# Attention with routed experts on one core: row places computed earlier, a third row per batch start on VectorE, output additions first, filler transposes, and new orders on all five engines

## The reference

```
xn  = layernorm(x)                                  # per token
q,k,v = xn Wq', xn Wk', xn Wv'                      # 32 query heads, 8 key heads, head size 128
q,k = rotary(q), rotary(k)
attn = softmax(causal(q k' / sqrt(128))) v          # 4 query heads share a key head
a   = attn Wo'
s   = softmax(xn router_w + router_b) + router_bias # 16 experts in 4 groups
keep the 2 groups with the largest maxima, then the 2 largest experts in them -> gate
y   = sum over experts of gate * ((silu(xn w1 + b1) * (xn w2 + b2)) w3 + b3)
z   = (silu(xn sw1 + sb1) * (xn sw2 + sb2)) sw3 + sb3
out = x + a + y + z
```

## Time and profile before

| what | value |
|---|---|
| median of 3 runs | 907.06 us (906.69 to 907.95) |
| the profiled execution, its own time | 905.59 us |
| its span | 903.8 us |
| PE busy | 888.5 us, 98% |
| DVE / ACT / POOL busy | 677.7 / 431.2 / 526.5 us |
| the loop over heads 1 to 6 | about 107.3 us a round |

### The profile page before, as it was taken

One profiled execution on the slowest core, in us unless ns is written; L12 is line 12 of the kernel. 1 busy time (PEld: TensorE's weight loads), 2 busy tenths in 40 slices (PEclk: granted clock), 3 DMA queues, 4 the chain that ended last, 5 costly groups with the idle time before them and its releaser, 6 DMA issues.

```text
span 903.8 us, 17478 instructions
## 1 busy us (share of the span) xinstructions
PE 888.5 (98%) x5066; PEld 762.2 (84%) x5066; DVE 677.7 (75%) x1614; ACT 431.2 (48%) x1083; POOL 526.5 (58%) x638
## 2 busy tenths in 40 slices
PE   8997999999999999999999999999999999999998
PEld 7786887888888888888888889888888888888886
DVE  6688876687767876768767786768776787676886
ACT  3504543554535644454554545445453564454543
POOL 5923786565654765538554575356565476543663
PEclk9999999999999999999999999999999999999999
DMA  9910223143223532335222443224322252230242
GB/s 329 319 47 15 92 94 123 42 131 121 88 76 86 172 95 79 90 99 168 87 87 76 114 163 87 75 81 126 123 87 75 89 172 94 80 92 22 84 150 94
DMA packets 52161, 97.73 MB, mean 108 GB/s; under 512 B 5920, under 2 KB 17824, under 8 KB 52128
## 3 DMA queue, kind: packets, MB, share of 16 engines
q1 hardware_dynamic: 49568, 88.94, 31.7%
q0 software_dynamic: 2560, 8.39, 2.8%
HBM read 74.76 MB, written 22.54 MB: 108 GB/s over the span
## 4 chain that ended last, share of the span: by engine, by line
PE 92%; DVE 5%; issue 1%; ACT 1%; DMA 0%; POOL 0%; SPq 0%; DVEq 0%
PE bank L1992 10%; PE bank L1990 10%; PE bank L1991 10%; PE bank L2190 7%; PE bank L2129 7%; PE bank L2131 6%; PE bank L2130 6%; PE bank L2226 6%; PE bank L2222 6%; PE bank L2223 6%; PE bank L2206 4%; PE bank L2203 4%; PE bank L2204 4%; PE bank L2251 1%; PE bank L2176 1%
## 5 line engine op out<-in xcount | busy, mean ns | idle before, releaser
L636 POOL TENSOR_SCALAR prob<-prob,rsum 128x128 f32<-128x128 f32 (+3 forms) x256 | 143.9, 582 | 89.8 <-DVE rsum L1480 89.1
L876 ACT ACTIVATE prob<-bank,nmax 128x128 f32<-128x128 f32 (+3 forms) x256 | 133.7, 528 | 113.9 <-DVE nmax L1474 111.3
L1474 DVE CUSTOM_DVE_ANT_0 bank<-bank,causal 128x128 f32<-128x128 f32 (+3 forms) x256 | 122.8, 501 | 35.5 <-PE bank L1992 33.7
L1502 DVE TENSOR_TENSOR pT_lo<-bank,pT_hi 128x512 fp32r<-128x512 f32 x160 | 109.1, 684 | 29.0 <-ACT pT_hi L896 28.6
L896 ACT ACTIVATE pT_hi<-bank 128x512 fp32r<-128x512 f32 x160 | 95.0, 596 | 67.1 <-PE bank L2190 53.4
L2222 PE MATMUL bank<-wo_lo,oT_hi 128*128 128x512 f32 x256 | 106.2, 415 | 0.0
L2129 PE MATMUL bank<-xT_hi,wq_lo 128*128 128x512 f32 x256 | 104.7, 409 | 1.5 <-DVE v_lo L1458 1.4
L619 POOL TENSOR_TENSOR w_lo<-w_raw,w_hi 128x1024 fp32r<-128x1024 f32 x31 | 74.3, 2398 | 52.7 <-ACT w_hi L931 52.7
L2131 PE MATMUL bank<-xT_hi,wq_hi 128*128 128x512 f32 x256 | 101.1, 395 | 0.0
L2226 PE MATMUL bank<-wo_hi,oT_lo 128*128 128x512 f32 x256 | 100.7, 393 | 0.0
L2130 PE MATMUL bank<-xT_lo,wq_hi 128*128 128x512 f32 x256 | 100.6, 393 | 0.0
(11 more groups left out here) (219 smaller groups left out, 2326.5 us busy)
## 6 DMA issues: line engine op xcount, KB each, us to landing
w_raw<-w SPq DMA_DIRECT2D x31, 512.0 KB, 3.5
wq_raw<-wq SPq DMA_DIRECT2D x32, 256.0 KB, 4.1
wo_raw<-wo SPq DMA_DIRECT2D x32, 256.0 KB, 2.8
xg<-x_slots SPq DMA_DIRECT2D x31, 256.0 KB, 3.5
w_raw<-w SPq DMA_DIRECT2D x31, 256.0 KB, 2.8
eb<-b SPq DMA_DIRECT2D x31, 256.0 KB, 3.9
y_slots<-eb SPq DMA_DIRECT2D x31, 256.0 KB, 2.5
x_slots<-pairs SPq DMA_DIRECT2D x3, 2048.0 KB, 16.0
```

Of the source, the lines that this page charges most:

```text
L636: last = nc.gpsimd.tensor_scalar(row, row, rsum[:, stat(b, i, h)], 1.0, ALU.mult, ALU.mult)
L876: last = nc.scalar.activation(prob[n % 2][:, h, 0:P * (i + 1)], bank[S_BANKS[use % 2]][:, 256 * k:256 * k + P * (i + 1)], ACT.Exp, bias=nm ...
```

## The change

The multiset of calls in the lists of the heads stays the same, save for what is named here.

1. Of the rows of batch 0, blocks 0, 1 and 2 are normalised on DVE and block 3 on ACT. For batch 1 it stays at two and two. A helper `wait_row` finds the semaphore of a row for PE and POOL.
2. The additions of the shared expert's result to row blocks 0 to 3 (`add_down`) all stand ahead of the choice of groups.
3. `count_blocks` and `first_blocks` leave the list of the first head on DVE. The first stands behind `lo_v(0, 0, 1)` ahead of the rotary steps of head 0, the second behind the first of these steps. `ranks` on PE moves with them, into the query projection of head 0.
4. `keep_busy(g, k)` on PE issues k transposes of the identity into a bank that holds nothing then; for g = 0 only: 9 behind the first scores, 5 ahead of `scores(0, 0, 1, 0)`.
5. All the lists of the heads on all five engines are in another order. In the list of the loop on PE `transpose_x` of the head's first tile is now first. `place_x(0, 0)` on POOL stands third among the calls of the first head that issue something, instead of eighth, and `place_x(0, 2)` behind the addition for the next head's queries; on ACT the `hi_wo` calls of the first head stand later.

```diff
+        DVE_ROWS, ACT_ROWS = (0, 1, 2, 4, 5), (3, 6, 7)
...
-                for n in (TB * b + 2, TB * b + 3):
+                for n in ACT_ROWS[b:2 * b + 1]:
                     nc.scalar.activation(xn[:, n, :], y[:, n, :], ACT.Identity, bias=lnt[:, 5, n:n + 1],
...
-                for n in (TB * b, TB * b + 1):
+                for n in DVE_ROWS[3 * b:3 * b + 3]:
                     nc.vector.tensor_scalar(xn[:, n, :], y[:, n, :], mv[:, n, 0:1], lnt[:, 2, n:n + 1],
...
             hidden(3)
-            for n in range(2):
+            for n in range(TB):
                 add_down(n)
...
-            for n in range(2, TB):
-                add_down(n)
...
             lo_v(0, 0, 1, FIRST_KV_BANKS[1])
+            count_blocks()
             for h in range(G):
                 turned = first_rot[h % 2]
                 turn_q1(0, 0, h, FIRST_Q_BANKS[h], turned)
                 turn_q2(0, 0, h, FIRST_Q_BANKS[h], turned)
+                if h == 0:
+                    first_blocks()
...
-                    (count_blocks, first_blocks, row_slots, row_gates, experts_of_tiles)[k]()
+                    (row_slots, row_gates, experts_of_tiles)[k]()
...
                 for c in range(HC):
                     project_q(0, 0, h, c, FIRST_Q_BANKS[h])
+                    if (h, c) == (0, 2):
+                        ranks()
...
-            def first_ranks(g):
+            def keep_busy(g, k):
 
                 if isinstance(g, int) and g == 0:
-                    ranks()
+                    for _ in range(k):
+                        nc.tensor.transpose(bank[OT_BANK][:, 0:P], ident[:, :], ident[:, :])
...
                 scores(g, 0, 0, 0)
-                first_ranks(g)
+                keep_busy(g, 9)
                 project_kv(g, 1, 0, 0)
                 scores(g, 0, 0, 1)
                 project_kv(g, 1, 0, 1)
+                keep_busy(g, 5)
                 scores(g, 0, 1, 0)
...
             def first_head(g):
                 exps(g, 0, 0, 0)
-                hi_wo(g, 0)
                 exps(g, 0, 0, 1)
-                hi_wo(g, 1)
                 hi_v(g, 1, 0)
```

More of the change, by code:

```diff
@@ L1185, in last_head @@
                 hi_pT(g, 1, 3, 3)
[L1186 removed]
+                exps(g, 1, 1, 0)
                 hi_oT(g, 1, 3)
@@ new lines, in first_head @@
+                transpose_k(g, 1)
+                values(g, 0, 1, 1)
+                transpose_p(g, 0, 2, 1)
+                project_out(g, 0, 0, 2)
+                project_q(g, 1, 2, 0)
+                project_q(g, 1, 2, 1)
+                project_q(g, 1, 2, 2)
+                project_q(g, 1, 2, 3)
+                transpose_p(g, 0, 2, 2)
+                scores(g, 1, 0, 0)
+                values(g, 0, 2, 0)
+                project_out(g, 0, 0, 3)
+                values(g, 0, 2, 1)
+                project_q(g, 1, 3, 0)
@@ new lines, in first_head @@
+                project_q(g, 1, 3, 1)
+                transpose_p(g, 0, 3, 0)
+                project_q(g, 1, 3, 2)
+                project_q(g, 1, 3, 3)
+                transpose_p(g, 0, 3, 1)
+                values(g, 0, 2, 2)
+                project_out(g, 0, 1, 0)
+                project_out(g, 0, 1, 1)
+                project_kv(g + 1, 0, 0, 0)
+                scores(g, 1, 0, 1)
+                values(g, 0, 3, 0)
+                project_kv(g + 1, 0, 0, 1)
+                transpose_p(g, 0, 3, 2)
@@ new lines, in first_head @@
+                project_q(g + 1, 0, 0, 1)
+                project_out(g, 0, 2, 2)
+                project_out(g, 0, 2, 3)
+                project_q(g + 1, 0, 0, 2)
+                scores(g, 1, 2, 1)
+                scores(g, 1, 2, 2)
+                project_out(g, 0, 3, 0)
+                project_q(g + 1, 0, 0, 3)
+                scores(g, 1, 2, 3)
+                transpose_p(g, 1, 1, 0)
+                values(g, 1, 0, 0)
+                project_out(g, 0, 3, 1)
+                project_kv(g + 1, 0, 1, 0)
@@ new lines, in first_head @@
+                project_out(g, 0, 3, 2)
+                project_kv(g + 1, 0, 1, 1)
+                transpose_p(g, 1, 1, 1)
+                project_out(g, 0, 3, 3)
+                scores(g, 1, 3, 0)
+                scores(g, 1, 3, 1)
+                project_q(g + 1, 0, 1, 0)
+                project_q(g + 1, 0, 1, 1)
+                project_q(g + 1, 0, 1, 2)
+                values(g, 1, 1, 0)
+                project_q(g + 1, 0, 1, 3)
+                project_out(g, 1, 0, 0)
+                scores(g, 1, 3, 2)
```

1296 lines of the change are left out of this document (618 added, 678 removed).

## The result

The changed kernel took 916.38 us (median), the kernel before 907.23 on the same chips. One of the four executions of the changed kernel took 3516 us; the ratio leaves it out and goes by the other three, 915.79 to 916.58: 1.0098, 95% interval 1.0078 to 1.0118. It is slower by 1%, outside of the range given. The profiled execution took 916.19 us, its span is 914.4, 10.6 more than before.

What follows compares the result with a forecast made beforehand. PE, busy 98%, was taken to bound the kernel. Terms -1.0 (start to 92), -1.3 (to 160), 0 (fillers), 0 (loop), +0.6 (last head) summed to -1.7: median 907.06 to about 905.3, range 902.6 to 908.9.

Steps and rivals of the forecast that it cites:

- The loop: Six rounds, 160 to 824 us: PE barely idle, can only lose; taken 0, bounds 0 and +0.65 a round, +3.9.
- Rival (c): Loop: each round's query projection meets a missing v_lo or kT_lo; 0.65 a round, +2.2 in all, 909.3; chance 0.15.
- Start: First rows normalised, edit 1: PE's 0.63 wait for xT_hi shrinks by some 0.34; taken -0.3, bounds 0 to -0.63.
- Output additions: Shared expert, edit 2: the 0.98 wait at 49.96 goes with the slow start of the matmul behind it; -1.1.
- Row places: DVE at 60 to 73 us, edit 3: count_blocks and first_blocks use up PE's lead; later waits shrink, row_slots takes back 0.2.
- the wait behind the table load: PE's wait at 77.60 in the first head stays, since a table load of 1.28 stands ahead of the first exps.
- the lead at 92: Start and edits 2 and 3 together: -1.0 at 92 us; wrong if not between 0.5 and 1.5.
- Fillers: First head, edit 4: fourteen transposes fit inside PE's idle time; taken 0, bounds 0 and +0.2.
- Second batch: First head, 92 to 160 us, edit 5: waits of 0.65 and 1.11 mostly shrink; -1.3, bounds -2.1 and +1.
- T1: Experiments' theory that the loop's new orders alone cost the time; it had the old-loop kernel 4.5 us faster than before.
- Last head: Edit 5 at the end: one wait of 1.6 for POOL's normalise, less waits that go; +0.6, bounds -1.5 to +1.6.

Runs made afterwards that it cites:

- A: Loop wait of PE's transposes for a bank lo_pT must read; changed kernel with hi_pT and lo_pT moved ahead of exps and maxima: round 108.85 (-0.76).
- B: Loop wait of project_out for y, the output bank; changed kernel with add_out(g,1,0) moved behind maxima(g,1,3,2): round 108.72 (-0.89).
- C: Loop wait of the query projection for kT_lo; changed kernel with ACT's hi_wo(g,3) moved behind hi_kT(g,1): round 109.52 (-0.1).
- The swap kernel with the first head of the kernel before: The kernel before with the changed kernel's loop lists on all five engines: 916.67 us against 904.23, ratio 1.0137, round 109.55.
- the one with the additions alone: The kernel before with all four output additions ahead of the choice of groups, nothing else: 905.08 us against 906.23, ratio 0.9989.
- the first head alone: The changed kernel with the kernel before's lists for the loop and the last head: 901.30 us against 904.77, ratio 0.9961.
- A, B and C moved: The changed kernel with four calls of the loop moved, for all three waits: 904.45 us against 904.23, ratio 1.0000.
- the kernel with the blocks late: The run with start and first head alone changed, with count_blocks and first_blocks moved behind all four rotary steps: 901.99 us against 901.30, ratio 0.9967.

## Why the prediction was wrong

It said 905.3 and the time was 916.4. The failed step is "**The loop.** ... Taken: 0. Bounds: 0 and +0.65 a round". A term put at nothing costs 2.28 us a round and 13.7 in all; with the old loop lists in its place the kernel is at 0.9984 of the one before, -1.6 us, where the sum without the loop was -1.7. That these two agree is partly luck: in the traces the terms without the loop come to -3.1, not -1.7. Step by step:

- Loop. I compared how much PE work lies between calls that depend on each other, found most distances longer, and took that for safety. Two things were wrong with it. I never set the distances against the length of the chain in the new order, which depends on what stands ahead of each link on ACT and DVE: the wait A comes from ACT standing at `exps` with a ready `hi_pT` behind it, and no distance on PE shows that. Nor did I look at what POOL does beside DVE: in the changed loop (160 to 824 us) 24 of 49 q_lo begin while POOL runs an elementwise instruction, and take 1.20 us in the mean; before it was 13 of 50, and 0.71. And the list of dependent pairs was short: it had no pair for the banks' way back, a transpose into a bank that `lo_pT` has yet to read (A) and an output projection into the bank that `add_out` has yet to empty (B). C is the one that I named, transposed keys to the next projection, and it is the smallest, 0.3 us a round in the trace; that moving its call gives anything is not shown. Rival (c) was right that there would be waits in every round, but its place was the query projection, which is C; at 0.65 a round it was too dear for C, and the two waits that cost most were in no rival.
- Bounds. "It can only lose" was in the text; an upper bound of one wait a round, of the smaller of the two sizes in the earlier trace rows, for lists of up to 158 calls in new order on five engines, had nothing behind it. The loop is run six times, so an unmended 0.3 us there outweighs any term of the start.
- Start, -0.3: right in size. First transposes to first product 2.37 us for 2.62; the wait of 0.63 is 0.36. The first transposes themselves came 0.14 later.
- Output additions, -1.1: right in kind, 1.35 alone.
- Row places, "-1.4 becomes +0.2 at 73": right, +0.39 at the key projection (73.35 for 72.96). The replay held up to the query projection, which came at 79.49 for the forecast 79.55, and the wait behind the table load stays as said: from the first scores to `scores(0, 0, 1, 0)` it takes 6.64 us in both kernels, and the fillers only hide it. The mis-sized part is what follows. I took 0.2 back for row_slots, and 0.6 more was gained, since this wait of the kernel before went:

```profile
89.77 0.44 PE L1990 MATMUL bank<-kT_hi,q_lo 128*128 128x384 f32 x1 [0.59 <-ACT prob L876]
```

So the lead at 92 is 1.9 and not 1.0, outside of the 0.5 to 1.5 that I had set as a sign of being wrong.
- Fillers, 0: right. The rule of the Trainium skill that I set beside it ("TensorE: Matmul & The Clock Gate", Part 4, about 275 ns for a transpose) would have made it +1.6; measured were 0.11 from start to start, and 0.27 us is how long one of them takes, so its figure is a duration here and not what one more costs.
- Second batch, -1.3: the trace gave -2.2, but the cause was misread. Both waits of the earlier trace rows come behind a DVE instruction that starts 1.2 and 1.3 us after PE's last matmul for it had ended. The swap kernel with the first head of the kernel before has neither (its window 130 to 160 below), the one with the additions alone has only one, of 0.62. So they do not follow from the order: they differ between traces of the same first head. That T1's -4.5 became -1.6 may have the same reason, if the kernel before runs without these waits on the chip where it takes 904.23 for 907.23. This is not shown, since that chip has no trace of it; and the first head alone gained 3.5, so how much of the -2.2 a timed run holds is left open.

```profile
130.00:160.00 30.00, 30.00 (x158) 25.16 (x157) 21.64 (x45) 11.80 (x29) 21.41 (x29) 1.00 0.31 116
```

- Last head, +0.6: right in place, +1.0 in size. The forecast had one wait of about 1.6 for POOL; there are three, 0.98 together, for the lo_pT behind combine_two and for POOL's normalise:

```profile
895.54 0.50 PE L2204 MATMUL bank<-pT_lo,v_hi 128*128 128x512 f32 x1 [0.43 <-DVE pT_lo L1504]
896.19 0.41 PE L2188 MATMUL bank<-ident,prob 128*128 128x128 f32 x2 [0.15 <-POOL prob L640]
897.01 0.44 PE L2188 MATMUL bank<-ident,prob 128*128 128x128 f32 x2 [0.40 <-POOL prob L640]
```

That step and the first head's up to 79.5 were replays, call by call, of what three engines have ahead of them; the loop's was not, and this is the difference between the steps that held and the one that fell.

What stays open: with A, B and C moved a round is 107.90, 0.57 above the old one, which no run takes apart; how much of A and B is the order of DVE and ACT alone and how much is POOL's splits beside q_lo; whether C is worth anything; and what makes the second batch's late starts come and go.

## What to carry to other kernels

Where an order is rewritten in a loop, replay the loop first, on every engine that hands something to the bound one, and include the buffers' way back (who must have read the bank before it is written again): busy shares and distances on the bound engine alone show neither. Look also at which instructions of GpSimd the new order puts beside VectorE's. An engine at half load can hold up one at 98% by waiting at the wrong call with a ready one behind it; look for idle time with a ready successor. And a wait that appears once in one trace is no term of a sum until a second kernel with the same lists shows it too.

## What the runs showed of the hardware

A DVE instruction that reads SBUF can be held until an instruction of POOL that runs beside it has ended. In the kernel with the first head alone, DVE and then POOL:

```profile
64.18 0.84 DVE L1386 TENSOR_TENSOR per_expert<-per_expert 128x16 f32<-128x16 f32 x1
63.97 1.01 POOL L669 TENSOR_TENSOR rot<-rot 128x384 f32<-128x384 f32 x1
```

In the kernel with the blocks late the same instruction, with POOL idle, takes 0.17 (at 75.92), and a one-input instruction on 128x16, also 0.17 elsewhere, is held:

```profile
73.17 0.95 DVE L1373 TENSOR_SCALAR iota<-iota 128x16 f32<-128x16 f32 x1
73.09 1.00 POOL L669 TENSOR_TENSOR prob<-prob 128x384 f32<-128x384 f32 x1
```

Both end 0.03 to 0.04 us behind POOL's. The first is 0.67 us on DVE's chain that the sum for `first_blocks` (1.05) did not have. Long instructions are held as well: in the loop of the changed kernel every q_lo (two inputs, 128x384) that begins 0.1 us or more after the start of an elementwise instruction of POOL that is still running ends 0.40 to 0.42 us behind that one's end, up to 2.45 us after its own start, and none of the others takes over 0.56. It goes the other way too: POOL's q_first takes 0.46 at 63.08 in the kernel with the blocks late, and 0.83 at 67.22 in the one with the first head alone, where a q_lo of DVE had begun 0.04 us ahead of it. Not every DVE instruction is held: in the same kernel a one-input TENSOR_REDUCE (L1385, at 63.73) takes its usual 0.42 while q_first runs.

The Trainium skill ("GPSIMD Engine Reference", 1. Specifications) says that GpSimd's SBUF interfaces are shared with VectorE and contended by its instructions with two SBUF inputs or in a 2-port mode. The trace agrees for two inputs; in which mode the one-input instruction ran, no trace shows.
